# Attention operand stacks loaded by one transfer each, and high parts written from ScalarE's queue

## What is computed

```python
x = x + _L0_attn_a_ref(_layernorm(x), ...)   # gated cumulative average, no softmax
x = x + _L0_ffn_ref(_layernorm(x), ...)      # two layers: "f0", "f1"
x = x + _L0_attn_b_ref(_layernorm(x), ...)   # "b"
x = x + _L0_ffn_ref(_layernorm(x), ...)      # two layers: "g0", "g1"

def _attn(x, wq, wk, wv, wo, bq, bk, bv, bo):        # in each layer of _ffn_ref
    q, k, v = ...                                    # 16 heads of 8
    att = jnp.einsum('bhqd,bhkd->bhqk', q, k) * hd ** (-0.5)
    att = jnp.where(causal, att, -jnp.inf)
    att = jax.nn.softmax(att, axis=-1)
    y = jnp.einsum('bhqk,bhkd->bhqd', att, v)
    return y @ wo + bo

# attn_b: q and k are multiplied once more by Wp (8 x 8) per head, no causal mask
scores = jnp.einsum('bnhi,bmhi->bnhm', q, k) / math.sqrt(D)
```

## Time and profile before

| | |
|---|---|
| time, median of 3 runs | 3047.06 us (3043.91 to 3050.0) |
| profiled execution | 3046.33 us |
| its span | 3044.6 us |
| granted TensorE clock, mean share | 0.938 |
| busy share PE / DVE / ACT / POOL | 87% / 85% / 74% / 21% |
| DMA: mean rate, packets | 39 GB/s, 109883 |
| loads of stacks, to landing (medians of the page) | 4.1 to 8.2 us |

### The profile page before, as it was taken

The page is one execution under the profiler, slowest core; times in us unless marked ns, Lnnn a source line. Parts: engine busy times, 40 slices in busy tenths (PEclk is TensorE's granted clock), DMA queues, the critical chain, the costliest instruction groups (busy, mean ns, idle before and its releaser), DMA issues. The chain is left out here.

```text
span 3044.6 us, 71512 instructions
## 1 busy us (share of the span) xinstructions
PE 2646.6 (87%) x28144; PEld 1160.3 (38%) x28144; DVE 2598.8 (85%) x3528; ACT 2249.2 (74%) x4330; POOL 637.5 (21%) x1177
## 2 busy tenths in 40 slices
PE   3679999899799995689999999589999898899976
PEld 3432333677323334322222222232334775333325
DVE  4789998787899985799999999598997887899976
ACT  1258988676589884369999999378887675688874
POOL 5233211544321011100000000132102433321011
PEclk8779999999799997889999999799999998899998
DMA  1141000224300000410000000510001223300001
GB/s 34 53 101 39 27 23 16 73 56 97 71 27 16 18 9 24 116 27 11 17 9 17 9 16 9 138 33 29 15 13 34 66 66 89 65 28 16 13 16 28
DMA packets 109883, 119.09 MB, mean 39 GB/s; under 512 B 20726, under 2 KB 87660, under 8 KB 109548
## 3 DMA queue, kind: packets, MB, share of 16 engines
q1 hardware_dynamic: 102444, 98.21, 12.2%
q0 software_dynamic: 4608, 13.96, 2.2%
q10 hardware_dynamic: 2496, 2.36, 0.3%
HBM read 70.31 MB, written 43.78 MB: 37 GB/s over the span
## 5 line engine op out<-in xcount | busy, mean ns | idle before, releaser
L1804 ACT ACTIVATE h_probsg<-h_ps_lowg 128x512 f32<-128x512 f32 (+3 forms) x812 | 424.5, 551 | 108.5 <-PE h_ps_lowg L1734 70.7
L1804 ACT ACTIVATE h_probsf<-h_ps_lowf 128x512 f32<-128x512 f32 (+3 forms) x812 | 424.4, 550 | 107.3 <-PE h_ps_lowf L1734 68.5
L1804 ACT ACTIVATE h_probsb<-h_ps_lowb 128x512 f32<-128x512 f32 x683 | 389.2, 596 | 61.0 <-PE h_ps_lowb L1734 46.2
L1755 PE MATMUL h_ps_valuesg<-h_probsg,v_all 128*9 128x256 f32 (+2 forms) x4608 | 350.2, 376 | 25.9 <-POOL h_probsg L1917 19.0
L1755 PE MATMUL h_ps_valuesf<-h_probsf,v_all 128*9 128x256 f32 (+2 forms) x4608 | 349.0, 375 | 26.0 <-POOL h_probsf L1917 19.3
L1755 PE MATMUL h_ps_valuesb<-h_probsb,v_all 128*9 128x256 f32 x4096 | 317.9, 382 | 7.9 <-ACT h_drainedb L1813 3.1
L1856 DVE TENSOR_REDUCE h_maxima_0b<-h_ps_scanb 128x2 f32<-128x1024 f32 x256 | 292.5, 1213 | 6.7 <-PE h_ps_scanb L1696 6.7
L1856 DVE TENSOR_REDUCE h_maxima_2b<-h_ps_scanb 128x2 f32<-128x1024 f32 x256 | 292.6, 1214 | 5.1 <-PE h_ps_scanb L1696 5.1
L1856 DVE TENSOR_REDUCE h_maxima_0g<-h_ps_scang 128x2 f32<-128x1024 f32 x224 | 258.9, 1216 | 19.8 <-PE h_ps_scang L1696 19.1
L1856 DVE TENSOR_REDUCE h_maxima_0f<-h_ps_scanf 128x2 f32<-128x1024 f32 x224 | 258.6, 1216 | 18.6 <-PE h_ps_scanf L1696 18.0
L1804 ACT ACTIVATE h_probsf<-h_ps_highf 128x512 f32<-128x512 f32 (+3 forms) x404 | 224.0, 554 | 35.0 <-PE h_ps_lowf L1734 32.3
(11 more groups left out here) (465 smaller groups left out, 5240.6 us busy)
## 6 DMA issues: line engine op xcount, KB each, us to landing
q_stack<-combine_weights SPq DMA_DIRECT2D x64, 256.0 KB, 3.7
q_stack<-in_L_ffn_e_w SPq DMA_DIRECT2D x24, 256.0 KB, 3.3
q_stack<-q_parts SPq DMA_DIRECT2D x22, 256.0 KB, 5.5
k_stack<-k_parts SPq DMA_DIRECT2D x22, 256.0 KB, 7.4
attended<-h_drainedf SPq DMA_DIRECT2D x16, 256.0 KB, 2.3
attended<-h_drainedf SPq DMA_DIRECT2D x32, 128.0 KB, 2.0
attended<-h_drainedb SPq DMA_DIRECT2D x32, 128.0 KB, 1.9
attended<-h_drainedg SPq DMA_DIRECT2D x16, 256.0 KB, 2.3
```

The source lines that it names most:

```text
L1755: last = nc.tensor.matmul(ps_values[32 * j:32 * j + VD, low:high], m.v_all[:, kb, QUAD * quad + j, :], probs[:, (u + j % banks) % RING_P, ...
L1804: nc.scalar.activation(by_head(probs[:, of % RING_P, :], of), by_head(ps_scores[of % RING_S], of), ACT.Exp, scale=SOFTMAX_SCALE).then_inc( ...
```

## The change

Three things. The order of the places is changed so that the six places can be read from the four in DRAM by one regular access pattern, three overlapping blocks of two places for queries and two overlapping blocks of three places for keys; each load of a stack half is now one transfer (`stack_rows`), in all five attentions. The writes of the high parts in `project_qkv` and `project_behind` (f0, b, g0) are issued by ScalarE right behind the two activations that make them; `EarlyProjection` keeps them on SyncE. And a group of four token tiles has its shifts moved by one transfer to both rows 48 and 112.

```diff
-Q_SLOTS = [0, 1, 2, 0]
-K_SLOTS = [2, 1, 0, 0]
+Q_SLOTS = [0, 0, 1, 2]
+K_SLOTS = [2, 0, 1, 0]
 SLOTS = len(Q_SLOTS)
-Q_AGAIN, K_AGAIN = 0, 1
-AGAIN = 2
-STACK = (SLOTS + AGAIN) * HD
+Q_RUNS, K_RUNS = (3, 2), (2, 3)
+STACK = 6 * HD
...
+def stack_rows(dram, runs, b, cols):
+
+    first = dram.rearrange("r (hp b) s -> r b hp s", b=2)[0:1, b, 0:1, cols]
+    count, places = runs
+    return bass.AP(first.tensor, first.offset, [[HD * HEADS * S, count], [HEADS * S, places * HD], [2 * S, PAIRS], [1, CH]])
...
         def load_stacks(queue, c, b):
...
                 queue.wait_ge(written[k][c % 2], 16 * 3 * (c // 2 + 1))
                 if c == CHUNKS - 1:
                     queue.wait_ge(v_ready, CHUNKS)
-                at = HALF * b
-                for n, first in ((SLOTS, 0), (AGAIN, again)):
-                    queue.dma_start(stack[at:at + n * HD, c, :, :],
-                                    dram.rearrange("r (hp b) s -> r b hp s", b=2)[first * HD:(first + n) * HD, b, :, cols])\
-                        .then_inc(arrived[b][c], 16)
-                    at += n * HD
+                queue.dma_start(stack[HALF * b:HALF * b + STACK, c, :, :], stack_rows(dram, runs, b, cols))\
+                    .then_inc(arrived[b][c], 16)
...
             for c in range(CHUNKS):
                 for part, ready in enumerate((high_ready, mid_ready, low_ready)):
                     for k in range(2):
-                        sp.wait_ge(ready, 2 * c + k + 1)
-                        write_part(sp, c, k, part)
+                        if part:
+                            sp.wait_ge(ready, 2 * c + k + 1)
+                            write_part(sp, c, k, part)
                     if part == 0 and 0 < c <= EARLY:
                         load_stacks(sp, c - 1, 0)
...
                         nc.scalar.activation(parts[:, c % 2, k, 0, :], projected(c, k), ACT.Identity, bias=bias[k])\
                             .then_inc(high_ready, 1)
+                for k in range(2):
+                    act.wait_ge(high_ready, 2 * c + k + 1)
+                    write_part(act, c, k, 0)
                 if c == 1:
                     load_stacks(act, 0, 1)
...
-        shift_moves.append((2 if tiles == TPC else 4) + (shift_moves[g - 2] if g >= 2 else 0))
-    arrived = 32 * (m.layers + 1)
+        shift_moves.append((1 if tiles == TPC else 4) + (shift_moves[g - 2] if g >= 2 else 0))
+    arrived = 16 * (m.layers + 1)
...
                 sp.wait_ge(freed, plan.turn_at[g] + 1)
+                if n == TPC:
+                    rows = slice(SHIFT_ROW, SHIFT_ROW + HALF + 1, HALF)
+                    sp.dma_start(m.q_stack[rows, c, 2 * quad:2 * quad + 2, :], shifts[0:4 * n, g % 2, :])\
+                        .then_inc(shift_in[g % 2], 16)
```

More of the change, by code:

```diff
@@ L682, in load_stacks @@
             cols = slice(c * CH, (c + 1) * CH)
-            for k, (stack, dram, arrived, again) in enumerate(((m.q_stack, m.q_dram, m.q_in, Q_AGAIN),
-                                                               (m.k_stack, m.k_dram, m.k_in, K_AGAIN))):
+            for k, (stack, dram, arrived, runs) in enumerate(((m.q_stack, m.q_dram, m.q_in, Q_RUNS),
+                                                               (m.k_stack, m.k_dram, m.k_in, K_RUNS))):
                 queue.wait_ge(written[k][c % 2], 16 * 3 * (c // 2 + 1))
@@ L1924, in shift @@
                 sp.wait_ge(freed, plan.turn_at[g] + 1)
+                if n == TPC:
+                    rows = slice(SHIFT_ROW, SHIFT_ROW + HALF + 1, HALF)
+                    sp.dma_start(m.q_stack[rows, c, 2 * quad:2 * quad + 2, :], shifts[0:4 * n, g % 2, :])\
+                        .then_inc(shift_in[g % 2], 16)
                 for b in range(2):
                     row = HALF * b + SHIFT_ROW
[L1927 to L1930, removed]
+                    if n < TPC:
                         for hp in range(2):
```

## The result

The changed kernel takes 3246.14 us (median of 4 runs, 3241.70 to 3254.74), the kernel before, on the same chip, 3046.98 us (4 runs, 3043.91 to 3050.00). The ratio is 1.0657, with a 95% interval of 1.0633 to 1.0681: 199 us slower, where 137 had been forecast. The profiled execution took 3245.97 us, its span 3244.2.

A forecast was written before the change was run, and what follows sets the result against it. TensorE and VectorE work was taken to bound the kernel, with transfers only 2% of the span. Losses of 32 + 37 + 29.5 + 39 = 137.5 us on 3046.3 gave 3184 us; forecast 3120 to 3230, outer range 3100 to 3320.

The forecast's parts named there:

- rival C: Loads narrow and dearer: 62 ns per piece, or issue that stops when one engine's queue is full; about 3290 us, chance 0.20.
- Engines by the outermost count: Stack loads: the side with the smaller outermost count decides, so three engines carry the queries' 384 pieces, two the keys'.
- Rival A: Stack loads stay 16 engines wide because the stack's 48 rows decide; about 3041 us, not slower; chance 0.13.
- B: Loads narrow, but each transfer gets engines of its own; 3139 us (chance 0.10) or 3055 us (chance 0.07).
- Items 1 to 3: Late loads, writes and shifts where stacks are built: 32 us lost in f0, 37 in b, 29.5 in g0.
- L: Engine 0's time for one half of one chunk, queries and keys, 320 pieces: 15.0 us (13.3 to 19.8).
- item 5: GpSimd's narrow loads of half 1 feed what is needed later: nothing lost, unless they fall on engine 0.
- the reservation about engine 0: If GpSimd's loads of half 1 fall on engine 0, more is lost, inside the range.
- Item 4: f1 and g1, each 19.5 us: 4.5 in the experts (late combine weights), 15 in the attention (late shift); 39 together.
- Item 6: Issue time: up to 5 us lost on ScalarE if uncovered, 2.5 gained on SyncE, 1.1 on GpSimd; sum taken as nothing.
- Item 7: A group's shift of eight rows on two engines instead of eight costs tenths of a microsecond.
- D: Loads narrow, but delays overlap idle time counted as needed; down to 3120 us, part of the forecast's 0.50.

The follow-up runs named there:

- gpsimd_later: Changed kernel with GpSimd's loads of chunks 2 and 3 issued 32 masking steps later in the four causal attentions; 3242.78 us, ratio 1.0643.
- gpsimd_narrow: Changed kernel with only GpSimd's loads (half 1, chunks 1 to 3) left narrow, all other loads wide; 3082.30 us, ratio 1.0112 to the kernel before.
- gpsimd_wide: Changed kernel with GpSimd's loads as three transfers of 16 rows (queries) and two of 24 (keys), SyncE's and ScalarE's still narrow; 3233.69 us, ratio 1.0615.
- one_shift: Kernel before with one edit: a group's shifts moved by one transfer instead of two; 3043.79 us, ratio 1.0000.
- narrow_loads_only: Kernel before with only the change's loads, one transfer of 48 rows each; high writes stay on SyncE, shifts stay two transfers; 3243.33 us, ratio 1.0648.

## Why the prediction was right, and where it was short

The measured 3246.14 us lies in the outer range of 3100 to 3320, but above the 3120 to 3230 to which I gave the chance of 0.50. That it is still inside is owed to the room left for rival C, whose price did not come true: the mechanism forecast is there, its sum is 62 us short, and the width of the range is what made up for that.

- **Engines by the outermost count**: right. Rates of 72 and 48 GB/s, 24 per engine, for counts 3 and 2; six engines at 6; sixteen at 16 with the loss gone. Rival A is out. By the Trainium skill ("DMA: Bandwidth & Descriptors", "Why a DMA increments its semaphore by 16 and not by 1") the number of engines is the largest up to 16 that divides both sides' slowest dimension; the new loads, with unequal sides of 3 or 2 and 48, agree.
- **Shared engines (against B)**: right. With SyncE's and ScalarE's loads both under way the rate of all queues together was 72 GB/s, three engines, and then 48. The pair of chunk 0 took 30.6 us in f0 until chunk 1 was written (forecast 32) and 28.9 in b (32); with ScalarE's load wide, 8.5 to 10.8 us came back in f0, b and g0. The same section of the Trainium skill says that transfers of the sync and scalar queues take the lowest-numbered engines; this agrees.
- **The signs named**: chunk 3's high parts came 18.0 us later (forecast 21), GpSimd's wait in g0 rose to 56.8 us (55), TensorE waited 31.1 and 20.0 us for shifts, and ScalarE's high parts of chunk 2 did not wait.
- **Items 1 to 3, short by 45.8 us (19.6, 16.0 and 10.2)**: the term L was mis-sized from chunk 1's load on. L = 15.0 us was about right while SyncE and ScalarE were alone (320 pieces at the 42.7 ns measured are 13.7 us). Behind that, GpSimd's transfers run too. The load of chunk 1 took 20.1 us in f0 (170.14 to 190.20, where the stopped issue ends) and 22.8 in b, that of chunk 2 in f0 21.3 until the next went out. gpsimd_later took 8.5 us out of f0's last two loads, and gpsimd_narrow shows 34 us with no narrow load of SyncE at all: item 5, nothing, was the step that failed. It erred twice. GpSimd's transfers slow SyncE's narrow loads beside them, and gpsimd_wide shows that for this they need not be narrow themselves; the reservation about engine 0 had room for it, the sum did not. And what GpSimd's loads feed is not always needed later: the first scan of a chunk waits for both halves of it, and in b of gpsimd_narrow GpSimd's landed last. And the writes of chunk 2, which I let land 2 us behind the load, could only be issued when it had drained, and took 6.2 us in f0 (190.20 to 196.44) and 6.6 in b, by the traces. In f0 the steps from the first load read 30.6 + 26.3 + 21.3 + 20.9 = 99.2 us where the forecast had 32 + 17 + 15 + 17 = 81: 18 of the 19.6. How the shortfall divides between GpSimd's share and the writes I read from the traces of f0 and b; it was run only for GpSimd's part in f0 and g0.
- **Item 4, short by 20 us**: the attentions of f1 and g1 lost 16.6 and 17.0 (15 forecast). In the experts I followed the combine weights of row 26 and not GpSimd's own load, which waits for chunk 1's writes ahead of the experts' next step: 12.48 us. With it out of the way the loss is 5.6 and 4.7, the 4.5 that was forecast.
- **Item 6**: nothing forecast, about 3 us lost, at the edge of what the runs can tell. **Item 7**: right, as far as one_shift can tell (ratio 1.0000, 0.9991 to 1.0009).
- **Rival C**: its mechanism is there and its price is not. Issue stopped for up to 18.8 us, but a piece took 42.7 ns and not 62, and ScalarE's stop cost nothing by narrow_loads_only; the reason I read for it is that SyncE's own writes of chunk 2 stood behind its next load anyway. SyncE's stop did cost: it is in the 6.2 and 6.6 us above. There was a sign before: I wrote that an issue took at most 0.82 us, which is the most of a shift's, while a key load in b took 1.29. **D** did not occur: no place lost less than was forecast.
- **A row misread**: the 120 to 395 GB/s of the signs are those of 142 to 170 us; in the earlier trace rows the lowest slice has 134.

16.6 us in the experts, 3.6 in the attentions of f1 and g1, 45.8 in f0, b and g0, less 3.8 elsewhere make the 62.2 us that the sum of 137.5 lacked.

## What to carry to other kernels

Before replacing two transfers by one, look at the outermost count of both sides: one issue of 0.6 us saved is worth nothing against a load that runs on 3 of 16 engines. When one queue's transfer becomes narrow, count all queues' pieces on its engines, GpSimd's too and also its wide ones, and list every instruction on any engine that waits for what is issued behind it, the loads of other queues among them. And an issue close behind narrow transfers can stand still for 10 us and more, so an engine that computes is the wrong one to make it; ScalarE's 13.6 us cost nothing here, by my reading only because SyncE's writes were later still.

## What the runs showed beside that

- An issue of 0.3 to 0.7 us took 10 to 18.8 us behind a narrow load, on SyncE and on ScalarE. L694 in the changed kernel (ns, least, median, most):

```profile
L694 SPq DMA_DIRECT2D q_stack<-q_parts x8: 716/726/18806, 139.5 to 1399.2; - x8
```

- GpSimd's narrow load cost it 1.31 and 1.68 us to issue (queries, keys) where two transfers had cost 1.12 each time (medians of 0.56), and q0 made 20448 packets for 14.22 MB instead of 4608 for 13.96.
- Six places instead of four in DRAM, half more written, gained nothing although the loads were one transfer each: 7 us slower with the high writes on SyncE's queue, level with them on ScalarE's.
